# One transformer block on one core: keys and queries stored whole and split later, half the weight pieces quantised in the first part, 20 small matmuls ahead of the group loop

## The reference, cut to what matters

```python
# x: (8, 1024, 512); 16 heads; 32 content + 16 rotated features per head; latent 128
h = layernorm(x)
c_q, c_kv = h @ W_DQ, h @ W_DKV
Q = concat(heads(c_q @ W_UQ), rope(heads(c_q @ W_QR)))         # 32 + 16 per head
K = concat(heads(c_kv @ W_UK), rope(h @ W_KR))                 # the rotated 16 shared by all heads
V = heads(c_kv @ W_UV)
s = where(causal, clip(Q @ K.T, -80, 80), -inf)
x = x + (softmax(s / sqrt(48)) @ V) @ W_O

q = fp4_quant_dequant                # blocks of 16: scale = max|.| / 6, round to 8 magnitudes
h = q(layernorm(x))
x = x + q(silu(h @ q(w_gate).T) * (h @ q(w_up).T)) @ q(w_down).T   # 512 -> 1408 -> 512
```

## Time and profile before

| | us |
|---|---|
| median of 3 | 3189.6 |
| the profiled execution | 3190.1 |
| its span | 3188.3 |
| part 1 and the way into part 2 (to the first score at 415.45) | 415 |
| part 2 (first score to the first instruction of part 3 on PE at 1413.49) | 998 |
| part 3 | 1775 |
| PE busy | 3043.1 (95%) |
| DVE busy | 2602.5 (82%) |
| ACT / POOL busy | 1222.3 / 668.1 |

### The profile page before, as it was taken

How to read it: one execution, slowest core, us unless ns; L and a number is a source line. 1 busy time by engine, 2 the same in 40 slices (tenths; PEclk the granted TensorE clock), 3 DMA queues, 4 the chain that set the end, 5 groups by cost and what they waited for, 6 DMA issues and landing times.

```text
span 3188.3 us, 65496 instructions
## 1 busy us (share of the span) xinstructions
PE 3043.1 (95%) x23492; PEld 2231.1 (70%) x23492; DVE 2602.5 (82%) x4427; ACT 1222.3 (38%) x1830; POOL 668.1 (21%) x634
## 2 busy tenths in 40 slices
PE   7999679999999999978999999999999999999999
PEld 6777534444444444447888888888888888888887
DVE  6777558888888888888888888888888888888886
ACT  3444346666666666653222222222222222222221
POOL 2434300000000000012233332332323223222332
PEclk9999889999999999989999999999999999999999
DMA  6999965665766657652000000000000000000000
GB/s 232 333 338 339 318 155 168 164 177 159 184 173 165 177 157 185 173 153 66 31 30 30 30 28 25 30 26 30 30 30 30 30 30 30 30 30 30 30 24 14
DMA packets 234506, 351.37 MB, mean 110 GB/s; under 512 B 17616, under 2 KB 117840, under 8 KB 234448
## 3 DMA queue, kind: packets, MB, share of 16 engines
q1 hardware_dynamic: 234448, 350.59, 36.4%
HBM read 205.55 MB, written 144.97 MB: 110 GB/s over the span
## 4 chain that ended last, share of the span: by engine, by line
PE 54%; DVE 1%; ACT 0%; issue 0%; POOL 0%; DVEq 0%
PE p_ring L1516 30%; PE p_ring L1544 15%; PE p_ring L1496 5%; PE p_ring L1534 2%; PE p_ring L1524 1%; DVE sb_wg_lo L1427 0%; PE p_ring L1556 0%; DVE sb_fp_tmp L102 0%; DVE sb_wd_lo L1427 0%; DVE sb_h_amax L88 0%; DVE sb_stage L1398 0%; DVE sb_ht_lo L1416 0%; DVE sb_xq L1373 0%; DVE sb_stats L1362 0%; DVE sb_xq L104 0%
## 5 line engine op out<-in xcount | busy, mean ns | idle before, releaser
L786 ACT ACTIVATE sb_probs<-scores 128x1024 f32<-128x1024 f32 (+3 forms) x768 | 586.2, 813 | 394.8 <-PE scores L970 384.2
L1516 PE MATMUL p_ring<-sb_wg_hi,sb_xq_hi 128*128 128x512 f32 (+1 forms) x1536 | 458.4, 379 | 0.3 <-DVE sb_wd_lo L1427 0.3
L1516 PE MATMUL p_ring<-sb_wg_lo,sb_xq_hi 128*128 128x512 f32 (+1 forms) x1536 | 448.5, 373 | 0.0
L1516 PE MATMUL p_ring<-sb_wg_hi,sb_xq_lo 128*128 128x512 f32 (+1 forms) x1536 | 447.9, 373 | 0.0
L845 DVE TENSOR_SCALAR sb_probs<-sb_probs 128x2048 f32<-128x2048 f32 (+3 forms) x320 | 288.3, 901 | 91.5 <-ACT sb_probs L786 88.5
L985 PE MATMUL ps_o<-sb_probs,sb_v 128*32 128x512 f32 (+3 forms) x3072 | 328.0, 499 | 0.0
L1232 POOL TENSOR_TENSOR sb_stage<-sb_stage,sb_h_inv 128x512 f32<-128x512 f32 (+1 forms) x192 | 210.7, 1098 | 542.2 <-DVE sb_h_inv L94 542.2
L970 PEld LDWEIGHTS scores<-sb_q_hi,sb_k_hi 32*128 32x128 f32 x1536 | 73.7, 182 | 345.1 <-ACT sb_probs L786 284.7
L1516 PEld LDWEIGHTS p_ring<-sb_wg_hi,sb_xq_lo 128*128 128x128 f32 x1536 | 285.3, 188 | 41.4
L1516 PEld LDWEIGHTS p_ring<-sb_wg_lo,sb_xq_hi 128*128 128x128 f32 x1536 | 284.8, 188 | 41.1
L1516 PEld LDWEIGHTS p_ring<-sb_wg_hi,sb_xq_hi 128*128 128x128 f32 x1536 | 277.0, 189 | 36.3 <-issue 0.7
(11 more groups left out here) (145 smaller groups left out, 5949.1 us busy)
## 6 DMA issues: line engine op xcount, KB each, us to landing
kq<-sb_kq_out SPq DMA_DIRECT2D x64, 1024.0 KB, 8.3
sb_xin<-in_L_attn_x_dram SPq DMA_DIRECT2D x32, 512.0 KB, 5.8
rq<-sb_r_out SPq DMA_DIRECT2D x32, 512.0 KB, 6.9
v<-sb_v_out SPq DMA_DIRECT2D x64, 256.0 KB, 6.0
sb_k_hi<-kq SPq DMA_DIRECT2D x32, 512.0 KB
sb_q_hi<-kq SPq DMA_DIRECT2D x32, 512.0 KB
sb_k_lo<-kq SPq DMA_DIRECT2D x32, 512.0 KB
sb_q_lo<-kq SPq DMA_DIRECT2D x32, 512.0 KB
```

Of the source, the lines that this page charges most:

```text
L786: act.activation(probs[:, k % PROBS, 2 * pair:2 * pair + 2, off:BANK], scores[(2 * k + pair) % RING2][:, :, off:BANK], ACT.Exp, scale=SCAL ...
L1516: i = pe.matmul(ps[:, m, 0:b0 - a0], xt[a][:, c, :], wg[b][:, m, c, a0:b0], start=(c == 0 and a == b == 0), stop=(c == DC - 1 and a == 1))
```

## The change

- kq holds keys and queries unsplit (two DMAs of 1 MiB per iteration instead of four); ACT's copy of a K or Q unit frees its PSUM slot, and DVE has no work on it. Part 2 loads them into one buffer `kq_raw`, a group ahead (`load_raw`); ACT rounds (`round_raw`, after steps 2 and 3), DVE subtracts (`rest_of_raw`, after the clips of steps 4 and 10), for the next group.
- Rotated features are stored as first and second halves: one unit R of 6 matmuls takes the place of R0 and R1. DVE multiplies 1024 columns twice, POOL's add and subtract and ACT's rounding have 1024 columns, the table in SBUF has four planes, and rq goes out in four DMAs of 256 KiB instead of two of 512.
- Unit C is two units, C0 (keys and values) and C1 (queries).
- Pieces 0 to 15 of the weights are quantised in part 1, one per iteration, on DVE alone, between X1 and R; pieces 16 to 31 in part 2, one per two groups, the first half of the steps in the even group and the second in the odd one.
- In part 2, `turn`, `invert`, `turn_back` and `normalise` of the first half of a group stand later (at steps 4, 10, 10 and 11).
- 20 matmuls of 32x32 stand on PE ahead of the first score.

```diff
-UNITS1 = ["C", "KR", "X0", "X1", "K0", "K1", "Q0", "Q1", "R0", "R1", "V0", "V1"]
+UNITS1 = ["C0", "C1", "KR", "X0", "X1", "K0", "K1", "Q0", "Q1", "R", "V0", "V1"]
 # part 1, SP body
-                sp.wait_ge(rope_lo, n * 3 + 3 + 3)
+                sp.wait_ge(rope_lo, n * 2 + 2 + 2)
                 for s in range(2):
-                    sp.dma_start(rq_v[s, b, :, :, cols], r_out[:, half, s]).then_inc(stored[half], 16)
-                sp.wait_ge(ps_free, unit(n, units.index("V1")) + RING1 + 1)
+                    for c in range(2):
+                        sp.dma_start(rq_v[s, c, b, :, :, cols], r_out[:, half, s, c]).then_inc(stored[half], 16)
+                freed(sp, n, "V1")
                 for j in range(4):
                     sp.dma_start(v_v[b, half * 4 + j],
                                  v_out[:, half, j].rearrange("p (g d) -> p g d", g=GROUPS)).then_inc(stored[half], 16)
+                if not last:
+                    sp.wait_ge(piece_ready, n + 1)
+                    sp.dma_start(piece_in[:], t["w_all"][n + 1]).then_inc(piece_loaded, 16)
+                sp.wait_ge(piece_done, n + 1)
+                sp.dma_start(t["wq_all"][n], piece_y[:]).then_inc(piece_stored, 16)
 # part 1, DVE body
-                    else:
-                        k, m = "KQ".index(name[0]), int(name[1])
-                        dve.wait_ge(act_hi, hi_count)
-                        pair = slice(2 * m, 2 * m + 2)
-                        dve.tensor_tensor(kq_out[:, half, k, 1, pair, :], ps[:], kq_out[:, half, k, 0, pair, :],
-                                          ALU.subtract).then_inc(ps_free, 1)
+                    if name == ("KR" if last else "X1"):
+                        dve.wait_ge(piece_loaded, n * 16 + 16)
+                        fp4_scales(dve, piece_in[:], piece_amax[:], piece_scale[:], piece_inv[:], piece_scaled,
+                                   n * SCALES_STEPS)
+                        ...
+                        dve.tensor_tensor(y, y, spread(piece_scale[:], WP // QB), ALU.mult).then_inc(piece_done, 1)
 # part 2, SP
+            def load_raw(it2, s):
+                g = it2 * 2 + s
+                sp.wait_ge(raw_split, g * 2 + 2)
+                for k in range(2):
+                    sp.dma_start(kq_raw[:, k], t["kq"][k, bass.ds(g * NI, NI)].rearrange("i p t -> (i p) t")
+                                 ).then_inc(raw_loaded, 16)
 # part 2, ACT and DVE
+                    if k in (1, 2) and not last:
+                        round_raw(*following(it2, s), k - 1)
...
+            def rest_of_raw(it2, s, k):
+                dve.wait_ge(raw_rounded, it2 * 4 + (s * 2 + k + 1))
+                dve.tensor_tensor((k_lo, q_lo)[k][s][:], kq_raw[:, k], (k_hi, q_hi)[k][s][:].bitcast(F32),
+                                  ALU.subtract).then_inc(raw_split, 1)
 # part 2, DVE, step 11
                     elif k == 11:
+                        normalise(it2, s, 0)
                         turn(it2, s, 1)
-                        own(dve, w_rounded, rounded + 3)
-                        dve.tensor_tensor(w, w, spread(w_scale[:], WP // QB), ALU.mult).then_inc(w_done, 1)
 # part 2, PE
+            for n in range(WARM_UP):
+                pe.matmul(ps_d[0:DH, 0:DH], ones[:], bound[:, 0:DH], start=True, stop=True)
...
                     pe.wait_ge(loaded[s], it2 * LOADS2 + LOADS2)
+                    pe.wait_ge(raw_split, it2 * 4 + (s * 2 + 2 + 2))
```

More of the change, by code:

```diff
@@ L411, in body @@
                         hi_count = n * len(HI1) + (2 + his.index(name) + 1)
[L412 removed]
+                    if name[0] == "C":
+                        k = int(name[1])
                         dve.wait_ge(act_hi, hi_count)
[L414 to L415 removed]
+                        dve.tensor_tensor(c_lo[:, k], ps[:, 0], c_hi[:, k].bitcast(F32),
+                                          ALU.subtract).then_inc(dve_free, 1)
+                        if k == 1 and not last:
@@ L475, in body @@
                 units = units_of(last)
-                his = [u for u in HI1 if u in units]
-                for name in units:
-                    number = unit(n, units.index(name))
+                for place, name in enumerate(units):
+                    number = unit(n, place)
                     ps = ring[slot(units, name)]
+                    if place >= RING1:
+                        before = units[place - RING1]
+                        (freed_last if last and before in FREED_BY_DVE else freed)(pe, n, before)
+                    else:
+                        freed(pe, n - 1, UNITS1[place - RING1])
                     if name[0] == "X":
@@ L625, in attention @@
         w_inv = sb("w_inv", [P, WP // QB])
-        w_loaded = [sem(f"w_loaded{s}") for s in range(2)]
+        w_loaded = sem("w_loaded2")
         w_scaled = sem("w_scaled")
@@ L717, in body @@
                 if not first:
-                    before = (it2, 0) if s == 1 else (it2 - 1, 1)
-                    store_piece(*before)
                     if not last:
@@ L723, in body @@
                         load(*following(it2, s))
-                    store(*before, 1)
+                    store(*preceding(it2, s), 1)
+                if s == 0:
+                    if not (isinstance(it2, int) and it2 == G2 - 1):
+                        sp.wait_ge(w_y, it2 + 1)
+                        load_piece(it2 + 1)
+                else:
+                    store_piece(it2)
+                if not (isinstance(it2, int) and it2 == G2 - 1):
+                    load_raw(it2 + 1, s)
                 if last:
@@ L930, in body @@
-                        dve.wait_ge(w_magic, piece + 1)
-                        dve.tensor_scalar(w_bits, w_bits, EXPONENT, TOP_MANTISSA, ALU.bitwise_and,
-                                          ALU.bitwise_or).then_inc(w_rounded, 1)
+                        add_up(it2, s, 1, 1)
                     elif k == 9:
-                        own(dve, w_rounded, rounded + 1)
-                        dve.scalar_tensor_tensor(out=w_tmp[:], in0=w_big[:], scalar=1.5, in1=w_all, op0=ALU.max,
-                                                 op1=ALU.add).then_inc(w_rounded, 1)
+                        if not last:
+                            rest_of_raw(*following(it2, s), 1)
```

322 lines of the change are left out of this document (184 added, 138 removed).

## The result

The changed kernel takes 3222.8 us (median of 4 runs, 3220.8 to 3225.3) against 3189.6 for the one before: a ratio of 1.0102, 95% interval 1.0090 to 1.0115. It is slower by 33 us. The forecast was 3215 us with a range of 3180 to 3252. The measured time lies inside, and the mechanism is the one that was forecast; that the sum comes as near as 8 us is in part luck, since two of its terms were off by 7 to 9 us each, with opposite signs.

A forecast was written before the change was run, and what follows sets the result against it. PE was taken to set part 1's pace, with DMA just short of it, and a chain of scores and exponentials part 2's. Terms +22 - 3 + 8 - 1 = +26 on 3190.1 us gave 3216, median 3215 us, range 3180 to 3252.

The forecast's parts named there:

- The ring through SP: Part 1: POOL's last subtraction, SP's stores and piece load, DVE, POOL and ACT form a closed wait of 23.5 us.
- Its two halves: Part 1: POOL's end to the piece's landing, 9.7 us, and from there to POOL's next end, 13.8 us.
- Against 22.1: +1.4 x 15: Part 1: a period of 23.5 us instead of 22.1 costs 1.4 us in each of 15 iterations, +21 us.
- The second ring: Part 1: the wait through POOL's inverse deviation for the next tokens, 20.9 us; as the pace-setting rival, chance 0.15.
- the port: Part 1: DVE and POOL exclude each other, adding up to 1.29 us and making the second ring 22.1 us.
- Into part 2: From part 1's end to the first score: 1 MiB less is loaded ahead of it, -3 us (0 to -5).
- The groups: Part 2: a product ahead of the turn that frees ps_d lengthens the group periods, +8 us (0 to +15).
- 0.7 later the load is at 702.56: 0.26 us per group: Part 2: the later turn delays PE's weight load, 0.26 us in each of 31 groups.
- The end of part 2: L944's 3.83 us leave DVE's tail; normalise and its wait for POOL come instead: -1 us (-3 to +1).
- PE's small matmuls: Ahead of part 2's first score: the 20 matmuls run in PE's wait for loads and cost 0.
- the chance of 0.05 for the fetch: Rival: PE's part 2 loop is fetched again each turn, 14 x 3 = 42 us on top, 3257 us; chance 0.05.
- a load that lands 5 to 6 us later: Rival in part 1: v stores stay slow, a ring of 26 to 28 us, 3250 to 3285 us; chance 0.10.

The follow-up runs named there:

- e7: The changed kernel with the load of the next piece and the store of this one ahead of SP's wait for POOL's last subtraction: 3185.0 us.
- e1: The changed kernel with the load of the next weight piece moved ahead of SP's wait for POOL's last subtraction, rq and v stores: 3199.5 us.
- e3: As e1, with POOL's inverse deviation for the next tokens between its addition and subtraction of the rotated queries: 3201.2 us.
- e5: The changed kernel with one more DVE product of 512 columns between normalise and turn at step 11 of every group: 3239.6 us.
- e10: As e7, with the inverse deviation in POOL's gap, ACT's key rounding right behind X1, and POOL's W_O subtraction in four parts: 3156.8 us.
- e4: As e1, with DVE's piece behind the products of unit R instead of behind unit X1: 3263.1 us.

## Why the prediction was right, and where not

- **The ring through SP** sets the pace: shown by the load moved ahead (-23 us) and one store back (+11.9). Its two halves were right to 0.4 us. Inside the first, two errors cancel: four rq stores took 2.8 us to issue and not 2.0, four v stores 2.7 and not 4.0; a store of 256 KiB took 0.55 us (rq) and 0.64 (v) at issue in the median, with the DMA share at 0.76. The landing took 3.9, not 3.5.
- **"Against 22.1: +1.4 x 15"** is the step that was mis-sized. The period came out at 23.89 over 14 iterations, +1.75 and not +1.4, since the ring was 0.39 longer than 23.5. And the last iteration was priced like the others. Before, it took 19.5 us, having no next tokens; in the ring it has nothing to leave out, DVE idles 9.28 us for its piece, and it takes 24.3: +4.8. A part's end must be priced by itself when the bound goes from work, which the last turn has less of, to a wait, which it has not.
- **The second ring** was given 20.9 us, with the port 22.1. With the first ring and the store's wait gone the period was 21.85, and the product was held up by 1.0 to 1.1 us in an iteration. By the Trainium skill (SBUF — State Buffer, Who interferes with whom) VectorE with two SBUF inputs and GpSimd exclude each other; the trace agrees (in e7 the product took 1.75 us beside POOL where it takes 0.71). It came in at full price only once nothing longer hid it.
- **The store of a piece** is a third ring that the forecast didn't list: the buffer piece_y is written anew each iteration and stored behind the same wait. In the changed kernel it is hidden by the load; in e1 and e3 DVE waited 0.2 to 3.0 us an iteration for it, and 6.0 and 7.1 in the last.
- **Into part 2**: -3 forecast, -2.6 measured.
- **The groups**: +8 forecast, +1.1 measured. The step "0.7 later the load is at 702.56: 0.26 us per group" took PE's weight load for the point at which the wait bites. It is the matmul: in the earlier trace rows the load at 701.87 was followed by a matmul at 702.30, so the turn that ended at 701.64 had some 0.6 us of room and not 0.2. With the product in front the turn ended 0.6 us later against PE's work and the load followed it by 0.06 us, not by 0.23. e5 shows where the room ends. ACT's roundings and DVE's subtractions cost nothing, as forecast.
- **The end of part 2**: -1 forecast, +1.4 for all that isn't the 31 periods. The lock moved from an operation that only DVE's tail stood behind to a clip on PE's path, a clip that the forecast did not look at, and PE then ran at the lower clock; e10 took 2.9 of PE's 3.47 us away by quartering POOL's subtraction.
- **PE's small matmuls**: "0", and for this pair of kernels it is 0, since both loops begin at good places. But the chance of 0.05 for the fetch, and its price of at most one load of 3.0 us a turn, came from a wrong reading: 37 packets show that a loop of this length is not fetched again from one place, and not that it isn't from another. A turn that is fetched again costs 8.2 us. Without the 20, the changed kernel would have been 145 us slower than the one before. By the Trainium skill (Runtime: NRT & Kernel Launch, Instruction fetch mechanics) TensorE holds 128 KiB, 2048 instructions, filled in blocks of 16 KiB, 256 instructions; the 16.3 KB per packet agree. The same section has a taken branch reach without a fetch only what is in two blocks; the trace disagrees for TensorE, a loop of some 1700 instructions runs with 37 packets in all. That 7 blocks are held and 8 are not is my inference from five starts (0 and 60 small matmuls bad, 8 and 20 good, and the kernel before); the block boundaries themselves no trace shows.
- **Small slips in the working** change nothing: 78 x 0.233 + 1.76 + 0.2 is 20.1 and not 20.2, the second ring with all of KR's 1.29 us is 22.2 and not 22.1, and a load that lands 5 to 6 us later than in a ring of 23.5 makes 28.5 to 29.5 and not 26 to 28.

What the change was worth without its waits: the same work takes 3156.8 us, 66 less than the changed kernel, with four edits, three that move instructions and one that splits an operation. The 33 us lost were not the price of the pieces in part 1, but of where their load, their store and the inverse deviation stand: with these three moved alone the time is 3173.1, 17 under the kernel before. Not tried: DVE's normalise beside POOL's subtraction (2.15 to 2.27 us in e10, 1.91 alone) kept apart as well; by the trace of e10, in which PE has no idle time there, it would gain nothing.

## What to carry to other kernels

When a change relieves the engine that sets the pace, walk every ring that closes over the in-order programs of two engines, the queue of stores included: buffers with one copy (piece_in, piece_y, rstd) that are refilled behind a wait for the end of the iteration are such rings, and each hides the next. Price a wait at the instruction that computes, not at the prefetch ahead of it, and price the last turn of a loop by itself. Look at the packets on the instruction queue of any kernel with a long loop: here 8 small matmuls ahead of it, 32 instructions, were worth 110 us.

## Not expected of the hardware

- The same loop cost 8.2 us more per turn when it began 80 instructions earlier or 160 later (20 small matmuls fewer or 40 more).
- The lock between DVE and POOL also held operations with one input: in e4 a TENSOR_SCALAR of 528 columns took 2.51 us where it takes 0.43, one of 33 columns 1.88 where it takes 0.18. A TENSOR_REDUCE beside POOL took its 0.69, and the split of X1, with one input in PSUM, its 2.48. The Trainium skill (SBUF — State Buffer, Who interferes with whom) fits all four: tensor_scalar can go into a mode with two ports, if its operands meet that mode's conditions, and then contends; tensor_reduce cannot on this chip; and an operation with at most one SBUF input outside such a mode does not contend. The forecast used only the rule for two inputs.
- A little idle time of PE can cost twice. In e1 it was idle 2.04 us, and in the transposes behind it the granted clock was 0.54, near the lower level, and they took 3.59 us. Others in the same run, behind 1.98 to 2.04 us of idle time, took 2.0 at full clock; what decides between the two is open. Five of e1's transposes were slow (2.7 to 3.6 us), and each stands in one of its five iterations of 23.2 us. PE's row and the window:

```profile
188.86 3.59 PE L496 MATMUL p_ring<-sb_ident,sb_xhat 128*128 128x128 f32 x16 [2.04 <-DVE sb_xhat L395]
```
```profile
188.80:192.50 3.70, 3.64 (x17) 3.62 (x18) 2.71 (x6) 1.09 (x3) 1.26 (x1) 0.54 1.01 322
```
